# One time-driven list schedule for all eight images in place of eight hand-written rounds with straight-line stages between them

## The reference, cut to what matters

```python
# B = 8 images; L = 32*32 patch tokens + 77 text tokens = 1101; D = 128
h = tok(x)                      # 5 shifted copies, 16x16 conv to 128, layer norm, dense 128x128
h = concat([h, txt], axis=1)    # 8 x 1101 x 128
h = h + attn(layernorm(h))      # 8 heads of 64, causal softmax, + its own input
h = h + ffn(layernorm(h))       # below
# ffn: x = x + depthwise conv of 3 along the tokens
#      q, k, v = x @ qkv_w.T + qkv_b, 8 heads of 16
#      logits = q k / sqrt(128);  idx = top_k(logits, 16)
#      out = softmax over those 16 only, times v, @ wo_w.T + wo_b
```

## Time and profile before

| | before |
|---|---|
| median of 3 runs | 5569.98 us (5568.24 to 5572.65) |
| profiled execution, its own time | 5581.88 us |
| its span | 5580.1 us |
| busy PE / DVE / ACT / POOL | 3848.1 / 3808.6 / 2759.8 / 2839.3 us |
| mean granted TensorE clock | 0.84 of full speed |
| DMA | 103.25 MB, mean 19 GB/s |

### The profile page before, as it was taken

One profiled execution on the slowest core, in us unless ns is written; L12 is line 12 of the kernel. 1 busy time (PEld: TensorE's weight loads), 2 busy tenths in 40 slices (PEclk: granted clock), 3 DMA queues, 4 the chain that ended last, 5 costly groups with the idle time before them and its releaser, 6 DMA issues.

```text
span 5580.1 us, 86720 instructions
## 1 busy us (share of the span) xinstructions
PE 3848.1 (69%) x32347; PEld 2582.3 (46%) x32632; DVE 3808.6 (68%) x5374; ACT 2759.8 (49%) x6137; POOL 2839.3 (51%) x3474
## 2 busy tenths in 40 slices
PE   4675777667777577757777577766777757773666
PEld 3444444444445344454444444444444534442444
DVE  1224887657874778738787488755788467873997
ACT  1442565435653456525565266543566346651444
POOL 2221666426663466616666166642666246661665
PEclk8877998878988789878998789887898878986676
DMA  3023001030201202030020300103020110003000
GB/s 52 3 30 50 3 9 24 5 51 2 31 1 27 28 3 31 1 53 2 3 31 1 54 3 11 21 5 50 2 31 1 33 22 2 3 1 51 1 1 5
DMA packets 221488, 103.25 MB, mean 19 GB/s; under 512 B 183616, under 2 KB 198544, under 8 KB 221072
## 3 DMA queue, kind: packets, MB, share of 16 engines
q1 hardware_dynamic: 221072, 97.68, 11.8%
HBM read 78.98 MB, written 18.67 MB: 17 GB/s over the span
## 4 chain that ended last, share of the span: by engine, by line
DVE 37%; PE 34%; ACT 13%; issue 7%; DMA 6%; POOL 2%; SPq 2%; DVEq 0%; ACTq 0%; POOLq 0%
PE causal_ps L716 10%; DVE A L1136 9%; DVE top L1131 9%; DVE top L1141 7%; PE out_ps L807 6%; ACT PB L998 6%; PE causal_ps L784 4%; DVE negmax L1153 4%; DMA H<-in_txt 4%; DVE A L1145 4%; PE logit_ps L742 3%; PE out_ps L835 2%; PE causal_ps L752 2%; ACT E L987 2%; ACT PT L932 2%
## 5 line engine op out<-in xcount | busy, mean ns | idle before, releaser
L601 POOL TENSOR_TENSOR A<-A,E 128x1101 f32<-128x1101 f32 x576 | 1378.9, 2394 | 0.8 <-issue 0.7
L1131 DVE MAX8 top<-logit_ps 128x8 f32<-128x1101 f32 x576 | 752.8, 1307 | 703.6 <-PE logit_ps L742 703.3
L932 ACT ACTIVATE PT<-causal_ps 128x512 f32<-128x512 f32 (+1 forms) x1728 | 820.7, 486 | 811.7 <-PE causal_ps L716 810.6
L716 PE MATMUL causal_ps<-ident,A 128*128 128x128 f32 (+1 forms) x5184 | 1031.6, 322 | 256.9 <-ACT PT L932 132.3
L590 POOL TENSOR_SCALAR A<-A 128x1101 f32<-128x1101 f32 x576 | 645.0, 1120 | 694.1 <-DVE A L1145 682.6
L716 PEld LDWEIGHTS causal_ps<-ident,A 128*128 128x128 f32 (+1 forms) x5184 | 681.0, 162 | 638.9 <-ACT PT L932 298.4
L987 ACT ACTIVATE E<-logit_ps,negtop 128x1101 f32<-128x1101 f32 x576 | 680.3, 1181 | 550.9 <-DVE A L1136 548.0
L595 POOL TENSOR_SCALAR negtop<-top 128x1 f32<-128x1 f32 x576 | 110.7, 192 | 1495.4 <-DVE top L1131 1469.6
L1141 DVE MAX8 top<-A 128x8 f32<-128x1101 f32 x576 | 753.2, 1308 | 11.3
L1136 DVE MATCH_REPLACE8 A<-top,logit_ps 128x1101 f32<-128x1101 f32 x576 | 746.0, 1295 | 0.9 <-issue 0.9
L1145 DVE MATCH_REPLACE8 A<-top,A 128x1101 f32<-128x1101 f32 x576 | 743.1, 1290 | 0.0
(11 more groups left out here) (140 smaller groups left out, 4127.9 us busy)
## 6 DMA issues: line engine op xcount, KB each, us to landing
stack<-qk_parts SPq DMA_DIRECT2D x128, 288.0 KB, 19.8
X<-in_x SPq DMA_DIRECT2D x248, 121.5 KB, 4.4
qk_parts<-OT SPq DMA_DIRECT2D x16, 864.0 KB, 5.2
Wp<-in_L_attn_W_in SPq DMA_DIRECT2D x96, 64.0 KB, 2.1
out<-H SPq DMA_DIRECT2D x8, 512.0 KB
stack<-in_L_tok_conv_w SPq DMA_DIRECT2D x30, 64.0 KB, 2.4
X<-in_x SPq DMA_DIRECT2D x8, 108.0 KB
H<-in_txt SPq DMA_DIRECT2D x8, 38.5 KB
```

Source lines behind the costliest of these rows:

```text
L601: nc.gpsimd.tensor_tensor(A[:, t % 3, :], A[:, t % 3, :], E1[:, t % 2, 0:L], ALU.add).then_inc(chosen, 1)
L716: last = nc.tensor.transpose(bank[0:w, 128 * j:128 * j + 128], src, ident[:, :])
L932: nc.scalar.activation(PT[0:rows, t % SLOTS, 512 * j:512 * j + 128 * len(tiles)], bank[0:rows, 0:128 * len(tiles)], ACT.Relu).then_inc(tur ...
L1131: nc.vector.max(top[:, t % 3, 0:8], logit_ps[:, 0:L]).then_inc(top8, 1)
```

## The change

All events of all eight images are entered in one `Plan`, each with an engine, a duration, a due time, the events it must follow, and the PSUM bank that it opens or closes. `arrange()` then walks a clock: whenever an engine is free it takes the ready event with the earliest due time, and gives a bank to one that opens one. What comes out is one fixed order for each engine, and each engine issues its own order, with semaphore waits on the events of the others. The engines have different orders now.

```diff
-def round_events(sparse, causal):
...
-ROUNDS = {kind: round_events(*kind) for kind in ((False, True), (True, True), (True, False))}
+STEP = 6.3
+IMAGE = TILES * STEP
+class Plan:
+    def add(self, engine, us, due, event, *behind, opens=None, closes=None, lag=0.12, long=False):
+        self.events[event] = [engine, us, due, list(behind), opens, closes, lag, long]
+    def arrange(self):
...
+                while ready[g]:
+                    item = ready[g].pop()
+                    e = item[2]
+                    _g, us, due, _b, opens, closes, lag, long = events[e]
+                    if opens is not None and opens not in owner:
+                        able = [b for b in range(BANKS) if free[b] is not None and free[b] <= now + 1e-9]
+                        if not able or (long and opened is not None):
+                            passed.append(item)
+                            continue
...
+def make_plan():
+    for c in range(B):
+        s0 = c * IMAGE
+        c0 = s0 - IMAGE
+        t0 = c0 - 30 * STEP
...
+        pace = 56 * STEP / len(fills)
+        def fill_due(n):
+            return c0 + 1 * STEP + n * pace
...
+        due = c0 + 58 * STEP
+        for t in range(NT):
...
+        for t in range(TILES):
+            due = s0 + t * STEP
+            first = due - 2 * STEP
+            add("PE", 0.5, first, ("logits", c, t), ("stack", c, t // QUARTER),
+                *([("exp_all", *tile(1))] if n else []))
+            add("DVE", 1.31, first, ("first", c, t), ("logits", c, t))
...
+PLAN = make_plan()
+ORDER = PLAN.arrange()
```

The buffers and engines change with it. `X` now holds 3 patch tiles and not 8, `stack` three quarters of an image:

```diff
-        X = sb("X", [128, NPT, U * UV])
+        X = sb("X", [128, 1 + X_SLOTS, U * UV])
-        stack = sb("stack", [128, 2, HF, LP], bf16)
+        stack = sb("stack", [128, STACKS, 2, HF // 4, LP], bf16)
-        H1 = sb("H1", [128, NT, D])
+        H1 = sb("H1", [128, 2, NT, D])
-        causal_ps = ctx.enter_context(nc.psum_tensor("causal_ps", [128, 4 * HALF], f32))
-        out_ps = ctx.enter_context(nc.psum_tensor("out_ps", [128, HALF], f32))
-        ring = [logit_ps, causal_ps]
+        score_ps = ctx.enter_context(nc.psum_tensor("score_ps", [128, 2 * HALF], f32))
+        bank_ps = [ctx.enter_context(nc.psum_tensor(f"bank_ps{b}", [128, HALF], f32)) for b in range(BANKS)]
-                    last = nc.vector.tensor_scalar(dst[:, t, :], src[:, t, :], mv[:, t, 0:1], rstd[:, t:t + 1],
-                                                   ALU.subtract, ALU.mult)
+                    nc.gpsimd.tensor_scalar(dst, src, rstd[:, k, i:i + 1], shift[:, k, i:i + 1], ALU.mult, ALU.add
+                                            ).then_inc(normal[k], 1)
-                    nc.vector.tensor_tensor(qkf[:, a, :], qkf[:, a, :], parts[:, a, 0, :], ALU.subtract
+                    nc.gpsimd.tensor_tensor(qkf[:, s, :], qkf[:, s, :], parts[:, s, 0, :], ALU.subtract
```

More of the change, by code:

```diff
@@ L65 @@
 BATCH = 4
+BATCHES = TILES // BATCH
 SLOTS = BATCH + 1
-PAIR_STEPS = TILES // NP
+X_SLOTS = 2
+STACKS = 3
+QUARTER = TILES // 4
 PB_SLOTS = 4
 PT_SLOTS = 4
-PER_STEP = 4
-def fours(items):
-    return [items[g:g + 4] for g in range(0, len(items), 4)]
-WG = fours(range(NT))
+BANKS = 3
+WG = [list(range(g, min(g + 4, NT))) for g in range(0, NT, 4)]
 def pieces(i):
@@ L238, with last_turn @@
[L238 to L254 removed]
+def last_turn(i, j):
+    return min(2 * j + 1, len(groups(i)) - 1)
@@ L477, in patches @@
                 start = x_flat[b].offset + (row * IMG * CH + j0 * P * CH - CH + e0)
-                return bass.AP(x.tensor, start, [[P * CH, G - j0], [IMG * CH, rows], [1, e1 - e0]])
-            def load_images(c, first=False):
-                for i in range(NPT):
-                    if not first:
-                        buf, n = fill(("XT", i), c - 1)
-                        sp.wait_ge(ring_done[buf], n + 1)
+                return bass.AP(x.tensor, start, [[P * CH, j1 - j0], [IMG * CH, rows], [1, UV - e0]])
@@ L529, in _ @@
-            load_images(0, first=True)
-            cycle(0, True, False)
-            for c in range(1, B - 1):
-                cycle(c, False, False)
-            cycle(B - 1, False, True)
-            store(B - 1)
-            sp.wait_ge(stored, B * 32)
+                        u0 = 1 if row < 0 else 0
+                        dst = X[32 * r:32 * r + 32, s, :].rearrange("p (u e) -> p u e", u=U)
+                        sp.dma_start(dst[1:G, u0:U, :], patches(c, row + u0, U - u0, 1, G, 0)
+                                     ).then_inc(x_loaded[s], 16)
@@ L538, in _ @@
+                if first_raw and event == "load_w" and (c, *of) == (0, 0):
+                    first_raw = False
+                    sp.wait_ge(setup_g, 4)
+                    load(rawT[:, 0:3, :], qkv_w.rearrange("(s p) n -> p s n", p=128))
+                    load(rawT[:, 3, :], wo_w)
+            for half in range(2):
+                sp.wait_ge(stored[half], B // 2 * 32)
         @block.gpsimd
@@ L634, in _ @@
-            for c in range(B + 1):
-                if c < B:
-                    halos(c)
-                rounds(c)
-        def fill_wait(pe, name, c):
-            buf, n = fill(name, c)
-            pe.wait_ge(ring_free[buf], n + 1)
-            return ring[buf], ring_done[buf]
-        def chunks(start, width):
-            cuts = [start] + [x for x in range(HALF, 3 * HALF, HALF) if start < x < start + width] + [start + width]
-            return list(zip(cuts, cuts[1:]))
+                pool.wait_ge(total_g, small[0])
@@ L651, in _, with chunks, turn @@
         @block.tensor
         def _(pe):
-            def transposes(dst, src_of, n, rows=128):
-                for t in range(n):
-                    last = nc.tensor.transpose(dst[0:rows, 128 * t:128 * t + 128], src_of(t), ident[:, :])
+            def chunks(start, width):
+                cuts = [start] + [x for x in range(HALF, 3 * HALF, HALF) if start < x < start + width] + [start + width]
+                return list(zip(cuts, cuts[1:]))
+            def turn(where, srcs):
+                for j, src in enumerate(srcs):
+                    w = src.shape[-1]
+                    last = nc.tensor.transpose(where[0:w, 128 * j:128 * j + 128], src, ident[:, :])
@@ L1220, in _, with settle @@
-            for c in range(B + 1):
-                if c < B:
-                    tokens(c)
-                rounds(c)
-                if c > 0:
-                    output(c)
-                if c < B:
-                    projections(c)
+            nc.vector.tensor_tensor(woB[:, :], bank_ps[0][:, 0:D], woB[:, :], ALU.add).then_inc(setup_done, 1)
+            small = {"ln": 0, "max": 0}
+            def settle(ins):
+                ins.then_inc(ln_v, 1)
+                small["ln"] += 1
+                dve.wait_ge(ln_v, small["ln"])
```

1809 lines of the change are left out of this document (1021 added, 788 removed).

## The result

| | before | changed |
|---|---|---|
| median | 5569.11 us (4 runs, 5565.5 to 5572.65) | 5127.9 us (4 runs, 5116.3 to 5131.91) |
| ratio | | 0.9204 [0.9187, 0.9221] |
| span of the profiled execution | 5580.1 us | 5122.9 us |
| mean granted TensorE clock | 0.84 | 0.88 |

The account below looks back on a forecast made before the run. DVE work was taken to set the least period, with DVE made to wait for logits. Start 496 + 7 x 516 + last image 402 + end 26 = 4536 us of span; + 2 - 12 = 4526 us, range 4253 to 4876.

Parts of the forecast that it names:

- The start, 496: Time until image 0's first scan: 496 us, between 455 and 540, including 20 us more for three patch buffers.
- The period, 516: One image's period: scans 384, causal DVE work 66, rest of the stage between rounds 16, waits 50; 516 us against 660.7.
- A: Rival: PE becomes the bound, at 87% busy; period 548, time 4750 us; chance 0.20.
- C: Rival: DVE's waits stay, only the stage between rounds is folded in; period 576, time 4946 us; chance 0.05.
- DVE's own work: DVE's busy time over the whole run, expected near 3625 us.
- its waits: DVE's waits in each period: half of some 100 us, so 50, between 0 and 100.
- POOL was right: POOL's load per period after gaining work from DVE: 382 us, or 74%; near 380 expected in the new profile.
- I leave this out: SBUF contention of POOL with DVE, priced at nothing; doubled conv instructions and small products would add some 20 us.
- Normalised tiles to POOL: Layer norm tiles moved from DVE: 6.9 us less DVE work per period, at nothing on the path on POOL.
- The last image, 402: Last image's sparse steps: 72 x 5.58 = 402 us, the step time of the kernel before.
- The clock: Granted PE clock: 0.9 or more between 500 and 4100 us, and 0.7 after that.
- rival B: DVE nearly saturated, waits under 10 us; period 455 to 465, time 4134 us; chance 0.10.

Follow-up runs that it names:

- e1_split: The changed kernel with each 31-partition patch transfer cut into one of 16 and one of 15 partitions, orders unchanged: 4467.36 us, ratio 0.8013.
- m_port: A kernel of its own without the computation: VectorE repeats each form twelve times, GpSimd idle, then adding 128x1101 tiles; with two SBUF inputs 2.31 us become 15.58.
- f4_neg_first: On top of e1_split, POOL's add of a step is placed behind the negation of the next step, orders planned anew: 4416.06 us, ratio 0.7921.
- m_shapes: A kernel that only loads patches, in series of one shape or by turns, its time not compared: 31 partitions take 6.8 us each, 32 take 0.64.

## Why the prediction was wrong, and where it was right

**The start, 496, measured 899: the failed step.** The sentence was "three patch buffers in place of eight, with a load in front of each tile (I take 20 us more at the start)". It priced the buffers and not the queue. The text on the change even says that patches take 8 transfers per tile, but no duration was put to them: in the trace of before, a whole load is a matter of 0.66 us, and the number of transfers looked harmless. The nearest row would have been no bound for the 31, whose price, by the rule cited above, depends on the factors of the partition count. What the forecast lacked was a rival of that kind: a transfer form that no row of before shows, on a queue that the first `stack` shares. It was worth 432 us at the start, and with the transfers mended the first scan is at 467, within the bounds of 455 and 540 given for it. Of the 587 us by which the span is longer than the sum had it (5122.9 and 4536), the start is 403, the periods are 137 and the last image 48.

**The period, 516, measured 535.6, and 502.9 with the transfers mended.** Of the difference of the two, 229 us in all, 196 lie at the borders. The forecast lies between the two. That 535.6 is still inside its bounds of 480 to 540 is luck: a stall at the borders that it didn't know of met waits that were shorter than it had them. Rivals A and C are out: PE is busy 416 of 495 us in a mended period and does not bound it. But 502.9 is the sum of two errors. DVE's own work was put at 3625 us in all and is 3787; its waits were put at 50 a period and are some 30 (DVE busy 474.7 in a period of 504). That e1_split comes within 1.3% of the forecast is therefore luck in part: start and periods came out 121 us shorter than forecast, the last image 50 longer. POOL was right, 382 us in the first period for a forecast of 380.

**"I leave this out", the second failed step.** The prediction weighed the rule of the Trainium skill (GPSIMD Engine Reference, Key points) on the shared SBUF interfaces, and let it go since the scans have one tensor input. The scans indeed did not stretch (medians of 1.29 to 1.31 us, before and after). But the sum has other instructions. The convolution and the small products were named and let go together with the scans; the minima were not named at all. Even an instruction of two numbers per row, if it has two SBUF inputs, waits until the running POOL instruction ends. In e1_split the minima are 91 us above 192 x 160 ns, the variances and Newton steps some 61, the two convolution instructions 14: 166 us, about the gap between 3625 and 3784. Doubling, the 20 us that the prediction tried, was far too little for an instruction of 0.16 us. The Trainium skill (Advanced Engine Details and Errata, VectorE Performance Modes) says that GpSimd instructions and VectorE instructions of a 2-port mode "will interfere/block eachother". The traces agree in both directions: m_port shows the held VectorE, the convolution in e1_split the held POOL. What would have warned was there: 18 variance and Newton instructions and 24 minima per image were to run in a period in which the forecast itself had POOL at 74%.

**Normalised tiles to POOL, "at nothing on the path".** Right for POOL: 448 ns a tile there, and PE's waits for them are 18 us in all. But the gain was taken as 6.9 us a period, 55 in all; undone, it costs 119. DVE's busy time grows by 71 of these, with tiles of 590 ns on average; the rest is idle time of DVE that no run explains.

**The last image, 402, measured 449.6.** It was taken over as if its order could not change. The order did, on POOL (the negation behind the sum) and on PE (the logits behind transposes that wait for the sum). With both as in f4_neg_first it takes 405.7.

**The clock** was right: 0.92 between 500 and 4100 us for a forecast of 0.9 or more (0.90 in the first period, whose border has 0.78), 0.70 in the last image, and 0.97 to 0.98 in periods of e1_split. The sign and the mechanism of the whole change were right too: the stage between rounds folded in beside the scans, and DVE's waits for logits fell from 703 us to 396, and to 181 in e1_split. With its transfers, its negation and its minima mended it takes 4274, where the forecast had 4526 and its rival B, DVE nearly saturated, 4134.

## What to carry to other kernels

Before moving work off the path by a new order, list every instruction form that the change adds, also those that look like bookkeeping, and ask of each DMA how many engines its partition count lets it use and what stands behind it in its queue: a slow transfer shows as the issue time of the next one. In an order in which VectorE and GpSimd overlap freely, count on every VectorE instruction that reads two SBUF tiles, and on a tensor_scalar from SBUF to SBUF, to last until the GpSimd instruction beside it ends, and try a reduction or an input in PSUM in its place. When an edit makes a planner plan anew, compare the orders of all engines before a gain is put down to the one line that was changed. And check a planner's prices: it had 0.9 us for a tile of loads that took 29.4.

## What the runs showed of the hardware

- Issued back to back, a load of 31 partitions of 18 runs of 216 bytes takes 6.8 us, and one of 32 partitions of 18 runs of 204 bytes takes 0.64 (m_shapes); the wait is on the queue of the next transfer, even if that is a single partition.
- Beside GpSimd sums of 2.57 us, twelve VectorE instructions with two SBUF inputs take 15.6 us and not 2.3, some two for each sum (m_port). A reduction, a reciprocal, MAX8 and a sum with a PSUM input take the same beside them as alone.
- GpSimd's sums are not slowed by these short instructions. Behind a VectorE instruction of 1.35 us with two SBUF inputs, a GpSimd instruction takes about 1.05 us more: a negation 1.25 us and not 0.19 (e1_split).
- Beside one-input GpSimd instructions of 1.19 us the same twelve with two SBUF inputs take 7.25 us.
